# Work between two mixture-of-experts layers taken in steps into the first layer's block loop, with that layer's pages numbered by group of four tiles

## The reference

```
x = x + xattn(ctx, layernorm(x), mask)              # 77 context rows per batch, 8 heads
x = x + ffn0(layernorm(x))                          # 8 experts of width 704, top 2, and a shared one of 352
x = x + hnet(layernorm(x), ctx)                     # rmsnorm(h) @ W_in + b_in + a scan over the context, by position
x = x + ffn1(layernorm(x))                          # 32 experts of width 128, top 6 of 4 of 8 groups, and a shared one of 512
```

## Time and profile before

| | us |
|---|---|
| median of 3 runs | 839.41 (837.9 to 843.5) |
| the profiled execution, whole | 839.12 |
| its span, first to last instruction | 837.3 |
| TensorE busy | 733.1 |
| VectorE busy | 419.2 |
| GpSimd busy | 309.4 |
| ScalarE busy | 276.7 |

### The profile page before, as it was taken

How to read it: one execution, slowest core, us unless ns; L and a number is a source line. 1 busy time by engine, 2 the same in 40 slices (tenths; PEclk the granted TensorE clock), 3 DMA queues, 4 the chain that set the end, 5 groups by cost and what they waited for, 6 DMA issues and landing times.

```text
span 837.3 us, 14535 instructions
## 1 busy us (share of the span) xinstructions
PE 733.1 (88%) x4703; PEld 638.2 (76%) x4703; DVE 419.2 (50%) x1622; ACT 276.7 (33%) x625; POOL 309.4 (37%) x328
## 2 busy tenths in 40 slices
PE   4999999989999999999999957899690999998865
PEld 3777788989999999999989945576470787886754
DVE  5998974223332322323323548788500455567653
ACT  2644533211111111111111213443330566666530
POOL 1332413730011111101101100777776477776650
PEclk9896978999999999999999975999995999999999
DMA  8999998257677777667753424766333776698966
GB/s 255 396 268 225 228 217 216 106 196 276 215 227 223 224 212 240 216 211 231 229 184 107 148 82 147 242 189 222 134 126 122 236 221 217 221 322 277 313 213 244
DMA packets 93241, 179.55 MB, mean 214 GB/s; under 512 B 9825, under 2 KB 54966, under 8 KB 93022
## 3 DMA queue, kind: packets, MB, share of 16 engines
q1 hardware_dynamic: 77760, 137.03, 55.1%
q0 software_dynamic: 13344, 38.68, 12.3%
q10 hardware_dynamic: 2046, 2.71, 1.1%
HBM read 132.43 MB, written 65.62 MB: 237 GB/s over the span
## 4 chain that ended last, share of the span: by engine, by line
PE 57%; DVE 13%; POOL 13%; issue 8%; DMA 5%; ACT 1%; SPq 1%; DVEq 1%; POOLq 0%; ACTq 0%
PE PB L594 21%; PE PB L619 12%; POOL rows_in L1893 8%; PE PB L810 6%; PE PB L821 5%; POOL sorted_x L1859 4%; PE PB L796 2%; PE PB L522 2%; DMA X<-in_x 2%; POOL rows_out L1905 1%; PE PB L686 1%; DMA MEM<-rows_out 1%; PE PB L576 1%; DVE WK L1274 1%; PE PB L606 1%
## 5 line engine op out<-in xcount | busy, mean ns | idle before, releaser
L594 PE MATMUL PB<-XT,MEM 128*128 128x128 f32 x1584 | 183.0, 275 | 0.6 <-issue 0.3
L594 PEld LDWEIGHTS PB<-XT,MEM 128*128 128x128 f32 x1584 | 179.7, 192 | 1.1 <-issue 0.6
L1868 POOL DMA_INDIRECT sorted_y<-WK x36 | 34.5, 958 | 260.0 <-DVE WK L1461 260.0
L1893 POOL DMA_INDIRECT rows_in<-MEM x96 | 93.2, 971 | 80.7 <-DVE MEM L1659 52.0
L619 PE MATMUL PB<-MEM,WK 128*128 x432 | 99.2, 379 | 0.0
L619 PEld LDWEIGHTS PB<-MEM,WK 128*128 128x128 f32 x432 | 79.3, 190 | 9.3
L927 ACT ACTIVATE XT<-PB 128x256 f32<-128x256 f32 x52 | 20.0, 384 | 168.6 <-PE PB L576 168.6
L810 PE MATMUL PB<-MEM,WK 128*128 128x128 f32 x456 | 64.6, 285 | 12.6 <-DVE WK L1769 8.3
L810 PEld LDWEIGHTS PB<-MEM,WK 128*128 128x128 f32 x456 | 56.2, 194 | 20.8 <-issue 14.4
L1905 POOL DMA_INDIRECT rows_out<-WS,MEM x58 | 57.8, 996 | 32.9 <-ACT WS L1066 19.8
L1438 DVE TENSOR_TENSOR WK<-WK,PB 64x128 f32<-64x128 f32 x36 | 10.5, 291 | 114.0 <-ACT WK L937 114.0
(11 more groups left out here) (260 smaller groups left out, 1244.3 us busy)
## 6 DMA issues: line engine op xcount, KB each, us to landing
MEM<-in_w SPq DMA_DIRECT2D x36, 896.0 KB, 7.0
rows_in<-in_consts SPq DMA_DIRECT2D x32, 600.0 KB, 13.5
MEM<-in_w SPq DMA_DIRECT2D x36, 512.0 KB, 4.0
MEM<-rows_in SPq DMA_DIRECT2D x58, 300.0 KB, 4.0
MEM<-rows_out SPq DMA_DIRECT2D x16, 768.0 KB, 7.5
MEM<-in_w SPq DMA_DIRECT2D x32, 256.0 KB, 2.9
MEM<-in_w SPq DMA_DIRECT2D x2, 3072.0 KB, 19.5
sorted_x<-MEM SPq DMA_DIRECT2D x1, 5070.0 KB, 40.7
```

The costliest lines, as they stand in the source:

```text
L594: t = e.matmul(o[:, to:to + P], UPW[m][i % (3 - m)][:, k, c * P:(c + 1) * P], XT[:, n % 2, k, :], start=(k == 0), stop=(k == 1))
L1868: e.indirect_dma_start(out=DY, out_offset=bass.IndirectOffsetOnAxis(ap=DEST[:, i:i + 1], axis=0), in_=YS[:, i % 2, :], in_offset=None).the ...
L1893: e.indirect_dma_start(out=DX1, out_offset=bass.IndirectOffsetOnAxis(ap=SLOT1[:, i, j:j + 1], axis=0), in_=XR[:, i, :], in_offset=None).th ...
```

## The change

Five things are changed.

1. **Pages by group.** The first layer's pages are numbered so that all rows of groups 0 to g are in pages below 8g + 15. A page that a group leaves part full is filled by the next one, so the number of pages stays the same. The counts are now taken per group (32 products with ones for 17), and the arithmetic from them to the slots is longer.
2. **Steps in the loop.** The work between the layers of a group is cut into eight steps (`mid(g, k)`, k = 0 to 7): 0 gather, add, statistics, norm, scale; 1 and 2 transposes; 2 and 3 `WIN` and patch products, adds; 3 second norm and scale; 4 transposes; 5 logits and Sigmoid; 6 picks; 7 ranks, shares, slots. Step k of group g stands in block 8g + 18 + k: group 0 in blocks 18 to 25, group 1 in 26 to 33, group 2 with step 0 in block 34 and steps 1 to 3 in the three late tiles.
3. **Order within a block.** TensorE runs a step after the first eight matmuls of `up(n)`; since the steps use banks 6 and 7, `up(n)` of a block with a step first waits for `y` of n - 2 and `xtb` of n + 1. VectorE and ScalarE run their parts partly before and partly after the block's own `hidden` or `gates`. A norm chain is done as a whole.
4. **After the loop** (`after_blocks`), for k = 0 to 7: one unit's `up1`, step k + 4 of group 2, one `down1`, step k of group 3; then the other units. SyncE loads two experts behind each `up1`. The units' sums are in banks 4 and 5.
5. **GpSimd** scatters group 0 inside the loop, four rows after each of the blocks 27 to 32, and the other 72 after it. `EARLY` is 13, `LATE` 3.

The diff, cut to its core:

```diff
-EARLY = 12
+EARLY = 13
+READY = tuple(8 * g + 15 for g in range(NR - 1))
+GATHER = {READY[g] + 2: g for g in range(NR - 1)}
+STEPS, LATE_STEPS, ROWS_AT = {}, {}, {}
+for g_ in range(NR - 1):
+    for k_ in range(8):
+        i_ = READY[g_] + 3 + k_
+        (STEPS if i_ < BLOCKS[0] else LATE_STEPS).setdefault(i_ if i_ < BLOCKS[0] else i_ - BLOCKS[0], []).append((g_, k_))
...
+def after_blocks(mid, up1, down1):
+    u = 0
+    for k in range(8):
+        up1(u)
+        if k + AHEAD < 8:
+            mid(2, k + AHEAD)
+        if u:
+            down1(u - 1)
+        u += 1
+        mid(3, k)
+    while u <= len(UNITS):
...
             def up(n, nb):
                 kind, i = item(n, nb)
+                steps = list(steps_of(n, nb))
+                if steps:
+                    q.wait_ge("y", n - 2)
+                    if n + 1 < EARLY + nb + LATE:
+                        q.wait_ge("xtb", n + 1)
...
+                            if c == 3 and m == 0:
+                                for g, k in steps:
+                                    mid(g, k)
...
             def down(n, nb):
                 kind, i = item(n, nb)
                 base, nch = 4 * IS0, 6 if kind == "b" else 3
                 q.wait_ge("h", n)
                 q.wait_ge("y", n - 1)
+                idle(7)
...
+                    steps = steps_of(n, nb)
+                    for g, k in steps:
+                        mid(g, k, False)
                     gates(n, nb)
+                    for g, k in steps:
+                        mid(g, k, True)
...
+                    steps = steps_of(n, nb)
+                    for late in (False, True):
+                        for g, k in steps:
+                            mid(g, k, late)
                     hidden(n, nb)
...
+            def mid(g, k, late):
+                a, b = GB[g], GB[g + 1]
+                b6, b7 = (6, 7) if g < 3 else (2, 3)
+                if k == 0 and not late:
+                    for i in range(4):
+                        q.wait_ge(f"ga{i}", a + i)
...
+                    for j in range(2):
+                        done = q.mark("gy", g) if j else q.mark("mid_v")
+                        e.tensor_tensor(X[:, a:b, :], X[:, a:b, :], GY[:, :, j, :], ALU.add).then_inc(*done)
+                        q.wait_ge(*q.last)
+                    for i in range(a, b):
+                        stats(i, "st2", "gy", g)
+                    norm2(g, "st2", RSQ_SCALE * (1.0 + EPS), RSQ_SCALE * EPS * EPS, "off1", g)
+                if k in (2, 3) and late:
...
+                if k == 6 and not late:
+                    picks(g)
+                if k == 7:
+                    if late:
+                        slots(g, b7)
+                    else:
+                        shares(g)
...
+            def block_iteration(n, nb):
+                scatter(n, nb)
+                kind, i = item(n, nb)
+                k = i - READY[0] - 12
+                if kind == "b" and 0 <= k < 6:
+                    rows_out(0, 4 * k, 4 * k + 4)
...
+            for g in range(1, NR):
+                rows_out(g, 0, 24)
...
+            def gather(g, last):
+                q.wait_ge("gy", g - 1)
+                q.wait_ge(f"ys{last % 2}", last)
+                q.wait_ge(f"ys{(last - 1) % 2}", last - 1)
+                for i in range(4):
+                    e.dma_start(GY[:, i, :, :], yd[GB[g] + i]).then_inc(*q.land(f"ga{i}", GB[g] + i))
...
+            def up1(n):
+                load_expert("u1", n)
+                load_expert("u1", n)
```

More of the change, by code:

```diff
@@ L83, in shape_constants @@
     c[:, CT6:CT6 + NT] = (np.arange(NT)[None, :] * P + np.arange(P)[:, None]) * TOPK + TRASH
+    c[:, CWR:CWR + 32] = np.tile(np.where(np.arange(8) == 7, -7.0, 1.0), 4)
     return c
@@ L91 @@
     "mid_copies": ("q1", "xp", "q2", "xta", "sc"),
-    "picks": ("grp", "smb", "cmb"),
+    "picks": ("grp", "smb", "cmb", "pads", "counted"),
     "slots": ("tup", "slot1", "base"),
@@ L224, in item @@
     return "s", n - nb
-def bank(i):
-    return (1, 3)[i % 2] if i < GB[1] else 2 + i % 3
 def place(i):
     return i % 5 if i < 10 else i - 5
[L235 to L263, removed]
-            up1(u)
[L265 to L286, removed]
@@ L562, in pe_program, with idle @@
                     f(k)
-            regs = {}
+            regs, busy = {}, {}
+            def idle(k):
+                if k in busy:
+                    q.wait_ge(*busy[k])
             def turn_x(n, nb):
@@ L574, in turn_x @@
                 q.wait_ge("lgc", 1)
+                idle(6)
                 for c in range(2):
@@ L645, in pe_program @@
             number = e.value_load(TAB[0:1, NBLK:NBLK + 1], min_val=0, max_val=P)
+            busy0 = dict(busy)
             def end0(c):
                 nb = BLOCKS[c]
-                last, count = EARLY + nb - 1, EARLY + nb + LATE
-                for n in range(SPLIT, count + 1):
+                busy.clear()
+                busy.update(busy0)
+                for n in range(SPLIT, EARLY + nb + LATE + 1):
                     block_iteration(n, nb)
@@ new lines, in dve_program @@
+            t = q.last
+            e.tensor_reduce(PAGE_G[:, 1:5], upto, AX.X, ALU.add)
+            e.tensor_scalar(PAGE_V, before, float(P), None, ALU.mult).then_inc(*q.mark("l0_v"))
+            q.wait_ge(*t)
+            e.tensor_tensor(LOWER, PAGE_N.unsqueeze(2).broadcast_to([P, 4, 8, 8]),
+                            CC[:, CLO:CLO + 64].rearrange("p (e f) -> p e f", e=8).unsqueeze(1).broadcast_to([P, 4, 8, 8]),
+                            ALU.mult).then_inc(*q.mark("l0_v"))
+            t = q.last
@@ new lines, in dve_program @@
+            q.wait_ge(*q.last)
+            e.tensor_tensor(PAGE_D, PAGE_O, PAGE_F, ALU.subtract)
+            pre = PRE.rearrange("p (g t) e -> p g t e", g=4)
+            tt0 = TT.rearrange("p (g t) e -> p g t e", g=4)
+            e.tensor_tensor(ge, pre, tiles(PAGE_V), ALU.is_ge).then_inc(*q.mark("l0_v"))
+            q.wait_ge(*q.last)
+            e.tensor_tensor(ge, ge, tiles(PAGE_D), ALU.mult)
+            e.tensor_tensor(tt0, pre, tiles(PAGE_F), ALU.add).then_inc(*q.mark("l0_v"))
+            q.wait_ge(*q.last)
@@ L1384, in dve_program @@
+            e.tensor_tensor(tt0, tt0, ge, ALU.add).then_inc(*q.mark("l0_v"))
             for k, a in enumerate((A1, A2)):
@@ L1624, in route @@
                 t = q.last
-                e.tensor_tensor(over_, loc, each(FREE), ALU.is_ge)
+                e.tensor_tensor(over, loc, each(FREE), ALU.is_ge)
+                e.tensor_tensor(tt, loc, each(CUR), ALU.add)
+                e.tensor_tensor(T32, tot, FREE, ALU.is_ge)
+                e.tensor_tensor(DELTA, FREE, CUR, ALU.add).then_inc(*q.mark("mid_v"))
+                t2 = q.last
+                q.wait_ge(*t2)
+                e.tensor_tensor(CUR, CUR, tot, ALU.add).then_inc(*q.mark("counted", g))
                 q.wait_ge(*t)
```

699 lines of the change are left out of this document (284 added, 415 removed).

## The result

The changed kernel takes 836.99 us (median of 20 runs, 831.91 to 842.91); the kernel before, in the same session, 840.96 us (20 runs, 837.46 to 846.13). The ratio is 0.9958, with a 95% interval of 0.9938 to 0.9978: it is 1.8 to 5.2 us faster, where 14.4 were predicted. The direction was right, the size was less than a third. Both traced executions have a span of 837.3 us, so the traces are compared stage by stage. The experiments ran on five chips: the first set on a quiet one, where the kernel before takes 839 us, the others on four slower ones, here A to D, where it takes 969 to 975 us and single engines stand still for up to 27 us for a releaser that the profile can't name; only ratios from the same chip are compared closely.

The account below looks back on a forecast made before the run. TensorE bounds the block loop, GpSimd's row scatters the stage between layers. Loop end 51.9 us later (4.7 + 17.9 + 26.3 + 3), second layer at 634.9 instead of 649.3: 839.1 - 14.4 = 824.7, forecast 825, range 808 to 845.

Parts of the forecast that it names:

- What goes: Between the layers: 24 scatters move into the loop, group 1's run during late tiles, only groups 2 and 3 hold GpSimd.
- Start of the loop: Ahead of the first block: longer page arithmetic on VectorE (+3.8 us) and 15 more small matmuls (0.9), uncovered, +4.7 us.
- TensorE work put into the loop: Block loop: step matmuls of groups 0 and 1, 8.95 us per group, nothing to hide them, +17.9 us.
- The new waits: Step blocks 18 to 34: TensorE waits before its up projection, 1.1 us in each of 17; bounds 0.65 and 1.6.
- Steps that are later than that: Loop blocks whose step answers come late: 3.1 us after step 0, 1.3 after step 3, 2.7 after step 7.
- rival 4: Block loop: VectorE's 57.5 us of steps is not hidden and reaches TensorE, +50 us, 875; chance 0.07.
- Clock: Block loop: the two waits of 3.1 us may each halve TensorE's granted clock for a while, +3 us.
- Late tiles: Three late tiles with steps 1 to 3 of group 2: last add 28.9 us after the loop's end, before 24.7.
- After the loop: From the last add to group 2's slots: 25.5 us, then 48 scatters, second layer at 634.9.
- rival 2: Behind the loop: group 2's slots later because three unit pairs run at 1.2 GHz, 10 us more, 835; chance 0.13.
- Hidden things: Behind the loop: group 3's slots hidden by 5 us, shared units and page table by 3.6, expert loads and gathers also.
- Rival 3: Block loop: TensorE's clock falls at every step block, 15 more waits at 1.6 us, +24, 849; chance 0.10.

Follow-up runs that it names:

- the exit edit: VectorE's part of group 3's step 0 put inside the loop's copies, ahead of the jump out, in the changed kernel; 0.9945 of the kernel before on the quiet chip.

## Why the predicted gain was too high

Two steps of the prediction failed, and they hold 10.5 of the missing 13.8 us: the price of the new waits in the loop was too low (4.8), and the way out of the loop's copies was left out of the term behind the loop (most of 5.7).

- *What goes.* Right. 24 scatters moved into the loop, 48 stand behind group 2's slots, and the end waits for the rows; putting the 24 back cost 11.8 us.
- *Start of the loop, +4.7.* GpSimd waited 19.23 us for its first slots where before it had been 15.60: arithmetic and the counts' matmuls together are +3.6 us, 1.1 less than said. The first block came 7.1 us later because this trace also reached that code 3.1 us later than that of before, in code that the change leaves alone. Over the traces of kernels with the same code up to there the first send lies between 138.0 and 144.6 us, so the 3.1 us are probably no cost of the change; of the kernel before there is one trace only, which can't settle it. They would stand for most of the difference between the 0.6 us of the two traces and the 4 us of the medians.
- *TensorE work put into the loop, +17.9.* Nearly right. With the waits out of the way the stretch from block 17 to block 35 is 165.3 us; before, it was about 140.7. The difference is 24.6, of which 5.1 are the four waits left: 19.5, that is 1.6 more than said.
- *The new waits: the first step that failed.* 17 blocks at 1.1 us, put together as 0.65 for the wait and 0.45 for the load. The wait was 0.68, the load 0.70. I took 0.45 as near 0.32, the idle time at the start of the copies, but that row was no load without cover: it stands behind two transposes of 0.41 us, and 0.41 + 0.32 is near the 0.70. The bound of 1.6 held the 1.38, the value in it was 0.28 too low, and 17 x 0.28 is 4.8 us. What the long waits cost beyond that was 1.7 us less than said: block 19 came 2.5 us late for 3.1, block 27 also 2.5, only those after step 7 more, 3.2 for 2.7. From the first block to block 35 the loop grew by 52.0 us where 47.2 were said. Less 19.5 of work and 3.1 of clock that leaves 29.4 for the waits, predicted 26.3. So that the loop's miss is just the 4.8 of the base waits is in part luck: the 1.7 and the 1.6 cancel.
- *Steps that are later than that.* The order of events was right: step 0 makes the next block wait for ScalarE's copy, step 7 for the result, step 3 adds 0.1 us, and no other step shows. VectorE's 50 us more in the loop are hidden, so rival 4 is out.
- *Clock, +3.* Two falls, 1.4 and 1.7 us, but only one behind a long wait; the other stands where the copies begin.
- *Late tiles.* 29.6 us for 28.9.
- *After the loop, 25.5: the second step that failed, and the largest single miss.* From the end of the last add it was 31.3 by the trace of GpSimd (31.7 from its start). I laid the steps end to end from the last add and put the way out of the copies at nothing: 3.85 + 1.07 us on VectorE, 2.07 on TensorE. The profile of before had such a gap in the same place, 3.02 us on VectorE, and I hadn't looked for it. With the gap covered it was 26.6. Two unit products at slow clock (3.49 and 3.13 us for 1.88) are the small piece of rival 2 that came true.
- *Hidden things.* On the quiet chip group 3's slots and the page table of the units were hidden as said. The table by an estimate of 2.7 us, for 3.6 said: its product began at 640.38, the rows were fetched at 645.55, and on chip A the fetch followed the product after 2.4 us. On the slower chips it was not hidden.
- *The rule on table loads.* The row of 567.15 + 1.28 with the sigmoid at 568.44 shows again a load and no second cost behind it; nothing here shows the drain that the Trainium skill, page "ScalarE: Activation LUTs", section "What ACT_TABLE_LOAD costs", adds.
- *Rival 3, the clock.* With all waits the loop stayed at a granted clock of 0.99. The Trainium skill, page "TensorE: Matmul & The Clock Gate", section "HAM oscillation — how this bites in real kernels", describes waits between short bursts, with each burst starting slowly. With the waits here, of 1.2 to 2.9 us of idle time, that was so at two of 17 step blocks.

Apart from the forecast's miss stands what the change could have given: of 34 us, 31 lay in the place of two waits. I priced them, at 26.3 us with the clock beside them, but took them as part of the change. Had I asked what each wait protects, the bank that the step writes, I would have seen that the eight matmul pairs ahead of it don't need it.

## What to carry to other kernels

A wait belongs just ahead of the first instruction that needs it, behind all work that doesn't; a wait at the head of a block stops the whole queue, and what is short behind it, here a register load, loses its cover and is paid in full, once per block. When a step moves to where it is hidden, look at what its waits stand in front of before counting its work. Behind a jump out of copied loop bodies look for engines that start late (here 3 to 5 us of VectorE in both kernels), and give the one on the critical path work ahead of the jump; and if two chains feed one queue in turn, moving one ahead only helps until the second is the late one.

## What the runs showed that was not expected

The load of one number into a register costs TensorE 0.70 us per block when it stands behind a wait, and nothing that shows when it stands ahead of it (block 17 to 18 in 9.10 and 8.40 us).

On four chips the kernel before took 969 to 975 us instead of 839, with the loop's blocks ahead of the steps unchanged at 7.72 us. Between the two traces of the changed kernel (span 837.3 and 968.6 us) 30 of the 131 us lie ahead of the first block, 5 in the loop, 22 in the late tiles, 34 between the layers and 41 in the second layer. Single stalls of up to 27 us are part of it, such as this one of VectorE among the late tiles, and in the second layer many of ScalarE, of 0.2 to 3.5 us; their releaser no row names:

```profile
600.44 0.69 DVE L1493 TENSOR_TENSOR X<-X,PB 128x512 f32<-128x512 f32 x1 [26.90 <-remote]
```

Such a chip changes what ends the stage between the layers, the page table of the shared units and not the rows, and so what an edit there is worth: the exit edit gave 0.2 to 0.7% there and nothing measurable on the quiet chip, though it took the same 4.4 to 4.7 us off the way to group 2's slots. What these stalls are was not tried.
